# Layer two of a two-layer transformer: sums of key blocks 0 and 1, and of 2 and 3, of the second query half made in pairs

## The chip, the cores and the metric

The kernel runs on one NeuronCore of one Trainium2 chip. The metric is the device time of one execution in microseconds (us), given as the median of several runs. Engines: PE is TensorE (PEld its weight loads), DVE is VectorE, ACT is ScalarE, POOL is GpSimd, SP is SyncE, which here issues DMAs.

## What is computed

Two layers, each an attention and a feed-forward part with a residual sum and a layer normalisation behind each. The change concerns the attention of layer two, which in short is this (two sequences of 1024 tokens, width 512, and per sequence 16 pairs of heads with 16 dimensions):

```python
scores = einsum('bhqd,bhkd->bhqk', q, k) * HD ** -0.5
scores = where(causal, scores, finfo.min)
probs = softmax(scores)
attn_out = einsum('bhqk,bhkd->bhqd', probs, v)
attn = attn_out[:, 0::2] - lambda_full * attn_out[:, 1::2]
```

So each of the 32 heads (16 in each of 2 sequences) has two components, each with scores of its own, that share one v of 32 columns.

## The kernel before

Layer two runs at 1621 to 2209 us of the span. A projection makes q, k and v, then 32 heads follow in `attention_phase` (called with `L1`).

**Work of a head.** The 1024 queries are two halves of 512 (`qc`), the keys eight blocks of 128 (`kt`). Under the causal mask the first half has key blocks 0 to 3 and the second 0 to 7, so there are 12 steps (`L.steps`): 0 to 3 for the first half, 4 to 11 for the second. Step 4 is key block 0 of the second half, steps 5, 6, 7 are blocks 1, 2, 3; steps 4 to 8 have all 512 queries, steps 9 to 11 have 384, 256 and 128. For each step and component:

- `score` (L626): a matmul with 50 rows, scores with keys down and queries across, into one of 3 banks of PSUM (`p_work`), taken in turn;
- `exp` on ACT (L816), into one of 4 probability buffers (`prob`, in `l_w_hi`);
- for the diagonal blocks (steps 0 to 3 and 8 to 11) POOL sets masked places to zero (L572);
- `sum_up` (L646): four products, v and a column of ones for both components, each into 32 columns of the array, added up in PSUM over the steps of a query half. TensorE runs each in two passes, so that a sum is 8 weight loads and 8 matmuls.

ACT copies the sums of a half (L769), TensorE turns them (`turn`, L696), DVE divides and combines.

**Maxima.** Before a head's scores are made, its queries' maxima must be known: `pair` (L604) makes scores with 48 rows the other way round into one of 4 banks (`p_ring`), and DVE reduces them (L883 without a mask; L880 with it, whose result is read out by a short second instruction). A head has 12 units of one 512-key piece or less, for 2 components: 24 matmuls and 24 reductions. TensorE makes them one to two heads ahead. DVE turns their maxima into a shift (L890), TensorE transposes it (`turn_shift`, L612), DVE copies it out (L897, L899). Turned sums and shifts use the banks of `p_ring` too.

Scores and maxima of component 0 use rows 0 to 63 of the array, those of component 1 rows 64 to 127. Below, a *score group* is an unbroken run of scores and maxima, which lies between sums or turns.

**Waits.** Every bank that is used again costs a wait, which stands ahead of the matmul on TensorE's one instruction stream:

```python
L593  pe.wait_ge(freed, L.freed_at[older])         # a maximum: the one 4 banks ago is reduced
L622  pe.wait_ge(exped, at - SCORE_BANKS + 1)      # a score: the one 3 banks ago is through exp
L640  pe.wait_ge(exped, 2 * (step + 1))            # sums of steps 4 to 7
L636  pe.wait_ge(out_copied, QC * n + qc)          # step 4: the first half's sums are copied
```

ACT's exp of step s waits for the sums of step s - 4 of the sequence (its buffer).

**Order.** A string of letters sets TensorE's order for each head (`Layer.heads`): Q and R take the next maxima of component 0 and 1, P both; U, V take the next score (components in turn), S two; W takes the next sum; X is the shift, T a turn. Sums run two steps behind the scores at the start of the string. DVE takes the maxima, shifts and turns in TensorE's order, ACT the exps in the order of the scores.

In the string before, the 5th to the 8th W are steps 4, 5, 6, 7, with a score group ahead of each: `WWW UUQRVQ W RUR W X QRUQUV W RUQUV W` (the first three W are steps 1 to 3, the X is a shift).

Of the kernel before, what the change touches and what calls it, by code (L numbers as in the profile page):

```python
# [31 lines left out]
B, T, D = 2, 1024, 512  # L32
# [50 lines left out]
class Layer:  # L83
# [141 lines left out]
    def k_head(self, n):  # L225
# [3 lines left out]

L0 = Layer("l0", D, D, False, "QRUWUQURUQDRUUUQRWUQUURQDRUUQRUWQUURUQWRUUQDXTWRUUUQRDQUURQUWRUUQURWQUURQUWRUU",  # L230
           24, (6, 12, 26))
L1 = Layer("l1", D // 4, D // 4, True, "PVRWSQVTQRVUVRWWWUUQRVQWRURWXQRUQUVWRUQVWUVURQRQWTQVRVUWWWQUV",
           20, (3, 2))


# [1318 lines left out]
def program(nc, A, out):  # L1554
    dram = lambda n, s, d: nc.dram_tensor(n, s, d, kind="Internal").ap()
    q_parts = [dram(f"q_parts{l}", (B * D // HD, PARTS * HD, T), F32) for l in range(2)]
    k_parts = [dram(f"k_parts{l}", (B * L.k_dims // HD, PARTS * HD, T), F32) for l, L in enumerate((L0, L1))]
    x0 = A["L0_attn_x"].rearrange("b t d -> (b t) d")
    out = out.rearrange("b t d -> (b t) d")
    with ExitStack() as ctx:  # L1560
# [60 lines left out]
        with ExitStack() as layer:  # L1621
            wo1_hi = layer.enter_context(nc.sbuf_tensor("wo1_hi", [P, KD, D], F32R))
            v_sb = layer.enter_context(nc.sbuf_tensor("v_all1", [P, NT * L1.v_dims], F32))
            early = ExitStack()
            early_q = early.enter_context(nc.sbuf_tensor("early_q", [P, 2, T], F32R))
            early_k = early.enter_context(nc.sbuf_tensor("early_k", [P, 1, T], F32R))
            wo = (wo_stage, Split(wo1_hi, wo_area.taken_by("wo_lo1", [P, KD, D], F32R)))
            attention_phase(nc, L1, xT, q_parts[1], k_parts[1], v_sb, attn_area, 2 * H_SIZE, neg_lambda[1][:, 0:1], C,
                            early_q[:, :, :], early_k[:, :, :], mean_sq, wo, norm_w[:, 1:2], [])
# [41 lines left out]
```

## Time and profile before

| | us |
|---|---|
| median of 3 runs | 2338.39 (2336.61 to 2339.71) |
| profiled execution, its own time | 2330.37 |
| its span, first to last instruction | 2328.6 |
| around the span | 1.8 |
| PE busy | 2240.8 (96%) |
| DVE busy | 1589.4 (68%) |
| ACT busy | 1241.2 (53%) |
| sums of layer two (L646), first to last start | 1673.5 to 2207.7 |

Busy time of an engine is the union of its instructions' spans; shares are of the span. The matmuls' spans are pipelined (each lasts on while later ones have started), so a PE at 100% is one without a visible hole. What a matmul or a sum costs is read from one start to the next start.

### The profile page before, as it was taken

The numbers are of one execution on the slowest core, as the hardware profiler recorded it, in microseconds if no ns is written. First come the engines' busy times: TensorE is split into PE (matmuls) and PEld (weight loads), VectorE is DVE, ScalarE is ACT, GpSimd is POOL, SyncE is SP. The second block draws the span as 40 slices with busy tenths as digits, with TensorE's granted clock in tenths as the row PEclk, the third lists the DMA queues.
The fourth block names the chain that finished last, engine by engine and source line by source line (L and its number), as shares of the span: only waits on it lengthen the run. The fifth ranks groups of instructions, "written<-read, shape, count | busy, mean of one in ns | idle before, by whom it ended". The sixth has DMA issues, their size and how long they took to land. (4 is left out here: it accounts for less than half of the span.)

```text
span 2328.6 us, 42022 instructions
## 1 busy us (share of the span) xinstructions
PE 2240.8 (96%) x14576; PEld 1292.5 (56%) x14576; DVE 1589.4 (68%) x3629; ACT 1241.2 (53%) x2486; POOL 930.9 (40%) x767
## 2 busy tenths in 40 slices
PE   8898999999999999799999999978999999999999
PEld 6663333333333333578888888857644444444377
DVE  3247899999999995554444443462589898889567
ACT  3116778787878787341222212251366666666644
POOL 4007888889999999510000000001011212121152
PEclk9999999999999999899999999989999999999989
DMA  6654322242223000220000000004702321220011
GB/s 221 154 131 52 83 29 29 29 55 30 29 29 51 7 2 2 69 73 28 1 27 27 27 27 27 1 1 127 153 14 37 44 43 29 37 44 2 2 46 55
DMA packets 59001, 109.00 MB, mean 47 GB/s; under 512 B 12028, under 2 KB 23292, under 8 KB 58808
## 3 DMA queue, kind: packets, MB, share of 16 engines
q1 hardware_dynamic: 57960, 103.39, 21.4%
q0 software_dynamic: 848, 3.15, 0.4%
q8 instruction: 107, 1.75, 0.3%
q14 instruction: 86, 0.70, 0.1%
HBM read 73.75 MB, written 31.46 MB: 45 GB/s over the span
## 5 line engine op out<-in xcount | busy, mean ns | idle before, releaser
L883 DVE TENSOR_REDUCE l_maxima<-l_p_ring 128x1 f32<-128x512 f32 x1280 | 814.2, 685 | 90.7 <-PE l_p_ring L604 73.3
L816 ACT ACTIVATE l_w_hi_prob<-l_p_work 128x512 f32<-128x512 f32 (+3 forms) x1280 | 600.1, 535 | 217.4 <-PE l_p_work L626 211.8
L604 PE MATMUL l_p_ring<-xT_all 48*128 48x512 f32 (+3 forms) x1680 | 490.8, 419 | 0.0
L626 PE MATMUL l_p_work<-xT_all 50*128 50x512 f32 (+3 forms) x1680 | 471.3, 417 | 0.0
L604 PEld LDWEIGHTS l_p_ring<-xT_all 48*128 48x128 f32 x1680 | 243.7, 186 | 334.2 <-DVE l_maxima L883 204.8
L558 POOL TENSOR_TENSOR l_part<-l_w_hi_prob,l_w_hi_prob 128x1024 f32<-128x1024 f32 x128 | 304.4, 2379 | 186.6 <-ACT l_w_hi_prob L816 147.7
L572 POOL TENSOR_SCALAR_AFFINE_SELECT l_w_hi_prob<-l_w_hi_prob 128x256 f32<-128x256 f32 x256 | 105.7, 419 | 515.8 <-ACT l_w_hi_prob L816 515.8
L558 POOL TENSOR_TENSOR l_part<-x_prob,x_prob 128x1024 f32<-128x1024 f32 x128 | 302.1, 2383 | 20.5 <-ACT x_prob L816 20.0
L626 PEld LDWEIGHTS l_p_work<-xT_all 50*128 50x128 f32 x1680 | 234.9, 185 | 130.0 <-ACT l_w_hi_prob L816 85.4
L816 ACT ACTIVATE x_prob<-l_p_work 128x512 f32<-128x512 f32 x512 | 275.3, 601 | 50.8 <-PE l_p_work L626 50.7
L646 PE MATMUL l_p_work<-l_w_hi_prob,v_all 128*32 128x512 f32 (+3 forms) x1536 | 301.3, 497 | 0.3 <-ACT l_w_hi_sums L769 0.2
L646 PE MATMUL l_p_work<-l_w_hi_prob,l_ones 128*32 128x512 f32 (+3 forms) x1536 | 301.1, 497 | 0.0
L880 DVE CUSTOM_DVE_ANT_0 l_masked_scores<-l_p_ring,l_mask 128x128 bf16<-128x128 f32 (+3 forms) x512 | 235.7, 487 | 49.4 <-PE l_p_ring L604 43.2
L1457 DVE SCALAR_TENSOR_TENSOR ffn_h<-ffn_p_u,ffn_group_scales,ffn_silu 128x512 f32<-128x512 f32 x64 | 48.1, 751 | 204.9 <-PE ffn_p_u L263 193.8
L1255 POOL TENSOR_SCALAR ffn_w<-ffn_w 128x1024 f32<-128x1024 int32 x21 | 24.2, 1174 | 409.0 <-DMA ffn_w<-in_L_ffn_down_w_T 409.0
L682 PE MATMUL l_p_ring<-l_part,l_ones 128*32 128x512 f32 x1024 | 136.9, 607 | 5.8 <-POOL l_part L558 5.8
L662 PE MATMUL l_p_work<-x_prob,v_all 128*32 128x512 f32 x1024 | 137.8, 611 | 0.0
L662 PE MATMUL l_p_work<-l_w_hi_prob,v_all 128*32 128x512 f32 x1024 | 137.4, 608 | 0.1
L1398 ACT ACTIVATE ffn_silu<-ffn_p_g,ffn_group_scales 128x512 f32<-128x512 f32 x64 | 44.0, 687 | 175.2 <-PE ffn_p_g L263 175.2
L1402 ACT ACTIVATE attn_h_hi<-ffn_h 128x512 fp32r<-128x512 f32 x64 | 40.4, 632 | 166.7 <-DVE ffn_h L1457 166.7
L960 DVE TENSOR_TENSOR l_part<-l_p_work,l_part 128x512 fp32r<-128x512 f32 x52 | 35.8, 691 | 135.7 <-ACT l_part L833 135.7
L646 PEld LDWEIGHTS l_p_work<-l_w_hi_prob,v_all 128*32 128x32 f32 x1536 | 70.6, 109 | 103.3 <-issue 57.9
(169 smaller groups left out, 3688.0 us busy)
## 6 DMA issues: line engine op xcount, KB each, us to landing
xT_all<-q_parts SPq DMA_DIRECT2D x180, 128.0 KB
q_parts<-l_part SPq DMA_DIRECT2D x64, 256.0 KB
xT_all<-k_parts SPq DMA_DIRECT2D x90, 128.0 KB
k_parts<-l_part SPq DMA_DIRECT2D x40, 256.0 KB
xT_all<-k_parts SPq DMA_DIRECT2D x90, 64.0 KB
ffn_w<-in_L_ffn_gate_w_T SPq DMA_DIRECT2D x8, 512.0 KB, 3.7
ffn_w<-in_L_ffn_up_w_T SPq DMA_DIRECT2D x8, 512.0 KB, 4.6
ffn_w<-in_L_ffn_down_w_T SPq DMA_DIRECT2D x8, 512.0 KB, 5.5
```

Source lines behind the costliest of these rows:

```text
L558: pool.tensor_tensor(pairs[room], prob[(step - QC) % L.prob_ring][:, :, :], prob[step % L.prob_ring][:, :, :], ALU.add).then_inc(paired, 1)
L572: pool.affine_select(out=part, in_=part, compare_op=ALU.is_ge, fill=0.0, base=0, pattern=[[0, 2], [1, P]], channel_multiplier=-1).then_inc ...
L604: filling = pe.matmul(p_ring[:, L.bank_at["maxima", n, u, sub] % L.ring, 0:keys], q[i][rows, n % 2, qt * P:(qt + 1) * P], k[i][rows, L.k_h ...
L626: pe.matmul(p_score[:, at % SCORE_BANKS, off:CH], k[i][rows, L.k_head(n), kt * P:(kt + 1) * P], q[i][rows, n % 2, qc * CH + off:(qc + 1) * ...
L646: summing = pe.matmul(p_out[r0:r0 + VD, off:CH], lhs, prob[step % L.prob_ring][:, sub, off:CH], start=first, stop=final)
L662: summing = pe.matmul(p_out[r0:r0 + VD, :], v, prob[(n * S + QC * kt + qc) % L.prob_ring][:, sub, :], start=kt == 0, stop=kt == KT - 1)
L682: summing = pe.matmul(p_ones[r0:r0 + VD, :], ones[:, :], added[:, sub, :], start=p == 0, stop=p == ONES_ROUNDS - 1)
L816: act.activation(prob[step % L.prob_ring][:, sub, off:CH], p_score[:, at % SCORE_BANKS, off:CH], ACT.Exp, scale=HD ** -0.5).then_inc(exped, 1)
L880: dve.tensor_tensor_reduce(masked_scores[sub][:, 0:keys], scores, mask[:, CH - keys:CH], 1.0, MASKED, ALU.add, ALU.max, to).then_inc(freed, 1)
L883: dve.tensor_reduce(to, scores, AX.X, ALU.max).then_inc(freed, 1)
L1398: act.activation(silu[i % 2][:, :], p_g[:, i % 2, :], ACT.Silu, scale=group_scales[par][:, 0, i:i + 1]).then_inc(silu_done, 1)
L1457: dve.scalar_tensor_tensor(out=h_full[i % 2][:, :], in0=p_u[:, i % 2, :], scalar=group_scales[par][:, 1, i:i + 1], in1=silu[i % 2][:, :], ...
```

## The change

One string is different: in each head, the sum of step 4 moves behind the following score group, to step 5, and that of step 6 moves behind the following group, to step 7.

```diff
-L1 = Layer("l1", D // 4, D // 4, True, "PVRWSQVTQRVUVRWWWUUQRVQWRURWXQRUQUVWRUQVWUVURQRQWTQVRVUWWWQUV",
+L1 = Layer("l1", D // 4, D // 4, True, "PVRWSQVTQRVUVRWWWUUQRVQRURWWXQRUQUVRUQVWWUVURQRQWTQVRVUWWWQUV",
            20, (3, 2))
```

No instruction is added or dropped: the rows of DVE, ACT, POOL and SP stay as they were, and on PE 2 of 12 sums a head move (16 of its weight loads, 16 of its matmuls).

TensorE around step 4 in a head of layer two (`l1_p_ring` are the maxima's banks, `l1_p_work` those of scores and sums, `l1_w_hi_prob0` and `prob1` the probabilities of steps 4 and 5; four rows of L646 are one sum):

```order
 L604 MATMUL l1_p_ring<-xT1_all_50,xT0_all_49 128x128
-L646 MATMUL l1_p_work<-l1_w_hi_prob0_20010,v_all1 32x512
-L646 MATMUL l1_p_work<-l1_w_hi_prob0_20010,l1_ones 32x512
-L646 MATMUL l1_p_work<-l1_w_hi_prob0_20010,v_all1 32x512
-L646 MATMUL l1_p_work<-l1_w_hi_prob0_20010,l1_ones 32x512
 L604 MATMUL l1_p_ring<-xT1_all_50,xT0_all_49 128x256
 L626 MATMUL l1_p_work<-early_q,early_k 128x512
 L604 MATMUL l1_p_ring<-xT1_all_50,xT0_all_49 128x384
+L646 MATMUL l1_p_work<-l1_w_hi_prob0_20010,v_all1 32x512
+L646 MATMUL l1_p_work<-l1_w_hi_prob0_20010,l1_ones 32x512
+L646 MATMUL l1_p_work<-l1_w_hi_prob0_20010,v_all1 32x512
+L646 MATMUL l1_p_work<-l1_w_hi_prob0_20010,l1_ones 32x512
```

The sum of step 4 now stands behind two maxima (256 and 384 keys) and the score of step 7, component 0; the sum of step 5 follows it at once.

TensorE around steps 6 and 7 of the same head (`prob2` holds the probabilities of step 6):

```order
+L604 MATMUL l1_p_ring<-xT1_all_50,xT0_all_49 128x512
+L626 MATMUL l1_p_work<-early_q,early_k 128x384
+L604 MATMUL l1_p_ring<-xT1_all_50,xT0_all_49 128x512
+L626 MATMUL l1_p_work<-early_q,early_k 128x384
 L646 MATMUL l1_p_work<-l1_w_hi_prob2_20012,v_all1 32x512
 L646 MATMUL l1_p_work<-l1_w_hi_prob2_20012,l1_ones 32x512
 L646 MATMUL l1_p_work<-l1_w_hi_prob2_20012,v_all1 32x512
 L646 MATMUL l1_p_work<-l1_w_hi_prob2_20012,l1_ones 32x512
-L604 MATMUL l1_p_ring<-xT1_all_50,xT0_all_49 128x512
-L626 MATMUL l1_p_work<-early_q,early_k 128x384
-L604 MATMUL l1_p_ring<-xT1_all_50,xT0_all_49 128x512
-L626 MATMUL l1_p_work<-early_q,early_k 128x384
```

Two maxima of 512 keys and both scores of step 9 (384 queries) now come ahead of the sum of step 6 and join the group before it; the sum of step 7 follows that of step 6.

## Rows read from the trace of the kernel before

**Rows 1.** Busy time by stage: us, busy (x count) of each engine, granted clock, DMA.
```profile
1650.00:1700.00 50.00, 45.08 (x298) 25.83 (x300) 29.86 (x97) 19.92 (x45) 4.90 (x12) 0.90 0.60 110
1900.00:2000.00 100.00, 100.00 (x936) 44.49 (x928) 89.53 (x302) 68.91 (x163) 19.85 (x48) 1.00 0.25 38
```

**Rows 2.** Timeline of PE, one head, steps 4 and 5: start, us, line, operation.
```profile
1900.26 0.50 PE L626 MATMUL l_p_work<-xT_all 50*128 50x512 f32 x2
...
1900.66 0.44 PE L626 MATMUL l_p_work<-xT_all 50*128 50x512 f32 x1
1900.84 0.22 PE L604 MATMUL l_p_ring<-xT_all 48*128 48x128 f32 x1
1901.05 0.62 PE L646 MATMUL l_p_work<-l_w_hi_prob,v_all 128*32 128x512 f32 x1
...
1902.04 0.38 PE L604 MATMUL l_p_ring<-xT_all 48*128 48x256 f32 x1
1902.05 0.49 PE L626 MATMUL l_p_work<-xT_all 50*128 50x512 f32 x1
1902.27 0.33 PE L604 MATMUL l_p_ring<-xT_all 48*128 48x384 f32 x1
1902.53 0.62 PE L646 MATMUL l_p_work<-l_w_hi_prob,v_all 128*32 128x512 f32 x1
...
1903.41 0.38 PE L612 MATMUL l_p_ring<-ident,l_shift 128*16 128x128 f32 x2
```

**Rows 3.** Timeline of PE, the same head, steps 6 and 7.
```profile
1903.72 0.56 PE L604 MATMUL l_p_ring<-xT_all 48*128 48x256 f32 x3
1904.07 0.63 PE L626 MATMUL l_p_work<-xT_all 50*128 50x512 f32 x3
1904.62 0.62 PE L646 MATMUL l_p_work<-l_w_hi_prob,v_all 128*32 128x512 f32 x1
...
1905.62 0.49 PE L604 MATMUL l_p_ring<-xT_all 48*128 48x512 f32 x1
...
1905.95 0.34 PE L626 MATMUL l_p_work<-xT_all 50*128 50x384 f32 x1
1906.23 0.62 PE L646 MATMUL l_p_work<-l_w_hi_prob,v_all 128*32 128x512 f32 x1
...
1907.22 0.39 PE L626 MATMUL l_p_work<-xT_all 50*128 50x256 f32 x2
```

**Rows 4.** Timeline of PE, the next head, up to its step 4.
```profile
1914.53 0.50 PE L604 MATMUL l_p_ring<-xT_all 48*128 48x512 f32 x2
1914.87 0.63 PE L626 MATMUL l_p_work<-xT_all 50*128 50x512 f32 x3
1915.11 0.40 PE L604 MATMUL l_p_ring<-xT_all 48*128 48x512 f32 x1
1915.44 0.51 PE L646 MATMUL l_p_work<-l_w_hi_prob,v_all 128*32 128x384 f32 x1
...
1917.65 0.62 PE L646 MATMUL l_p_work<-l_w_hi_prob,v_all 128*32 128x512 f32 x1
```

**Rows 5.** Timeline of ACT, the head of rows 2: copy of sums, then exps.
```profile
1900.39 0.60 ACT L769 ACTIVATE l_w_hi_sums<-l_p_work 128x512 f32<-128x512 f32 x1
1900.89 0.59 ACT L816 ACTIVATE l_w_hi_prob<-l_p_work 128x512 f32<-128x512 f32 x1
...
1904.50 0.60 ACT L816 ACTIVATE l_w_hi_prob<-l_p_work 128x512 f32<-128x512 f32 x1 [1.25 <-PE l_p_work L626]
1904.99 0.59 ACT L816 ACTIVATE l_w_hi_prob<-l_p_work 128x512 f32<-128x512 f32 x1
```

**Rows 6.** Timeline of DVE, the same head: where reductions with a mask are read out.
```profile
1901.74 0.08 DVE L880 DVE_READ_ACCUMULATOR2_ANT l_maxima<- 128x1 f32 x1
...
1905.04 0.08 DVE L880 DVE_READ_ACCUMULATOR2_ANT l_maxima<- 128x1 f32 x1
```

**Rows 7.** Timeline of PE's weight loads, the third score of rows 2.
```profile
1900.60 0.19 PEld L626 LDWEIGHTS l_p_work<-xT_all 50*128 50x128 f32 x1
```

## The prediction

> **What bounds the kernel now.** I read the busy time by stage first, to see which engine sets the pace of layer two's heads. In 100 us of it PE is busy for 100.00, DVE for 89.53 and ACT for 68.91, at a granted clock of 1.00 (2.4 GHz) [rows 1]. Then the timeline of PE: the sum of step 4 starts at 1901.05 and again at 1917.65, so a head takes 16.60 us [rows 2, 4], and 32 of them some 531 us. PE has no hole that shows, so a head's time is the sum of what PE's instructions cost from start to start, and only what shortens PE's stream or puts a wait into it counts. The timelines of ACT and DVE, read last, say when a bank comes free; the reader is to hold those times against the starts on PE.
>
> **What is saved: two changes of work a head.** A sum that a score group follows takes 0.99 us (1901.05 to 1902.04; 1906.23 to 1907.22), one that the shift follows, which is of the same kind (narrow columns), 0.88 (1902.53 to 1903.41) [rows 2, 3]. So a sum that another sum follows is worth 0.88, 0.11 less. A group pays at both its ends: a 512-wide matmul costs 0.34 as the first of its half of the array (1914.53 to 1914.87), 0.24 in the middle (to 1915.11) and 0.33 as the last (to 1915.44) [rows 4], which is 0.10 and 0.09 for the ends. A pair of sums in place of two single ones thus saves 0.11 + 0.10 + 0.09 = 0.30 us. Two pairs in each of 32 heads: 19 us, if nothing waits. The Trainium skill has the reason for these ends, in TensorEngine Tiling (Array Packing), Key Properties: a change of tiling mode drains TensorE. The rows agree with it, and by that rule alone the time would fall by the 19 us; that is the first rival.
>
> **What is added: the sums were the cover of waits.** Today a single sum stands between two score groups and lasts about 1 us, in which DVE reduces maxima and ACT takes exps out of the banks that the next group wants. The change takes that 1 us away ahead of both groups; what waits stands ahead of everything else on PE's one stream, both sums included. I work out each place by its last wait. Prices: from the end of the work that frees something to PE's start 0.06, as the sum of step 4 shows, which waits for the copy that ends at 1900.39 + 0.60 = 1900.99 and starts at 1901.05 [rows 2, 5]; from a weight load within a group to its matmul 0.06 (1900.60 to 1900.66) [rows 7, 2].
>
> *Step 4.* Its group now runs on: 256-key maximum, score of step 7 (component 0), 384-key maximum. If nothing waited, they would follow the 128-wide maximum of 1900.84 within some 0.2 us. But:
> - the score of step 7 uses the bank of the score of step 5, component 1, whose exp ends at 1900.89 + 0.59 = 1901.48 [rows 5];
> - the 384-key maximum uses the bank of the last 512-key maximum made before the 128-wide ones, which DVE has read out at 1901.74 + 0.08 = 1901.82 [rows 6]. This wait ends last.
>
> Both are set by earlier PE work that stays where it is, and DVE works without a hole there, so the change does not hasten them. The matmul starts at 1901.82 + 0.06 + 0.06 = 1901.94. From it to the sum behind it today's 0.26 (1902.27 to 1902.53) [rows 2] holds: sum of step 4 at 1902.20, step 5 at 1903.08, the shift at 1903.96, where it is 1903.41 now. **0.55 us later.**
>
> *Step 6.* I count from the start of the shift, S, as the reductions and exps there follow from work behind S. The group today starts at S + 0.31 (1903.72) with three maxima and three scores [rows 3]; the two maxima and two scores of the next one now join it. The last two must wait:
> - the second 512-key maximum for the bank of the 256-key one behind the shift, read out at 1905.04 + 0.08 = 1905.12, S + 1.71 [rows 6];
> - the first score of step 9 for the exp of step 7, component 1, which ends at 1904.50 + 0.60 = 1905.10, S + 1.69; the second for that of step 8, component 0, which ends at 1904.99 + 0.59 = 1905.58, S + 2.17 [rows 5]. This ends last.
>
> The second score starts at S + 2.17 + 0.06 + 0.06 = S + 2.29; with today's 0.28 from it to the sum (1905.95 to 1906.23) [rows 3] the sum of step 6 starts at S + 2.57, step 7 at + 3.45, and with 0.99 the next group at S + 4.44. Today that is 1907.22 - 1903.41 = S + 3.81. **0.63 us later.**
>
> So a head is 0.55 + 0.63 = 1.18 us longer, the saving included. Once PE is later, the waits in the rest of the head become shorter, and none is on its path today; nothing gives the loss back, and PE's steps behind keep their lengths. Of 32 heads I count 31, since in the last one no maxima are left to be made and the first of the two waits is a lighter one: 31 x 1.18 = 36.6, taken as **+36 us**.
>
> What costs nothing: the instructions are the same ones. The exps of steps 8 and 10 wait for the sums of steps 4 and 6, which now end later; but the first exp of step 8 would start at about S + 1.58 (1904.99 - 1903.41), long behind the sum of step 4, and scores of step 10 come only behind step 7's sum. The copy of the first half's sums is no longer waited for (a few hundredths, inside the working). DVE and POOL wait for nothing that moved later than their own banks, and SP's queue has nothing moved past it.
>
> **Bounds.** Below: with neither the 0.06 of the wake-up nor that of the load the places give 0.43 and 0.51, 29 us. Above: if a load behind a wait costs as much as one at a group's start, 0.10 (above), and one more wake-up falls in each place, it is 0.10 more in each, 1.38 a head, 43 us. I take the middle, since its prices are those of a wait and a load in this very place.
>
> Against its own time the profiled execution would go from 2330.4 to 2366; the median of the runs shown lies 8.0 above it, which gives 2374.
>
> **Rivals.**
> 1. *It gets faster.* The saving stands and the banks come free in time: 2338.4 - 19 = 2319. That needs PE to pass a waiting score and run the sums, or DVE and ACT to be ahead. For it: halves of the array do pass one another (three maxima start from 1903.72, the third of which is behind a score in the program, and the scores only from 1904.07) [rows 3]. Against it: that is passing what waits for its half, not for a semaphore, and the last reads of both places lie some 0.8 us and more behind the time at which the group wants the bank; DVE at 90% has no such lead [rows 1]. It decides at 0.55 and 0.63 us: if the frees came earlier by more than these, the kernel would be faster. Chance 0.06. On the other side the Trainium skill says in TensorEngine Tiling (Array Packing), PSUM Bottleneck, that tiling hastens TensorE and not the emptying of PSUM, which may then be the bound. By it the change has nothing to gain in either place; the rows of DVE and ACT above agree.
> 2. *One place only.* One of the two waits is covered, for instance because PE's delay in one place gives DVE and ACT a lead in the other. The covered place then saves its 0.30, or comes out even where half a wait is left: a head is longer by 0.25 to 0.33, or by 0.55 to 0.63, 31 of them by 8 to 20 us: 2346 to 2358. For it: DVE is idle a little ahead of the shift's copies. Against it: the last wait of the second place is ACT's, counted from the shift itself. Chance 0.08.
> 3. *The two cancel.* Waits of 0.30 where I work out 0.85 to 0.93: no change, 2338. No row gives such a value. Chance 0.03.
> 4. *The clock falls too.* PE now stands still for up to half a microsecond four times a head. In the stage ahead of the heads, where PE is busy for 45.08 of 50 us, the granted clock is 0.90, a mixture of both levels (1.2 and 2.4 GHz) [rows 1]. A clock of 0.97 would add 3% of 531 us, 16 us: 2390. Against it: the holes are short beside those of that stage. Chance 0.04.
>
> **How the numbers follow.** The forecast has 0.79; its own range is 2367 to 2381. Rival 2 at its upper end and half of what lies between are taken in below, a little of rival 4 above: 2355 to 2384 leaves out rival 1, rival 3, the lower part of rival 2 and rival 4, together near 0.2. A measurement of this kernel can tell some 0.2%, 5 us, from no change. Faster by more: 0.07. Within: 0.03. Slower: 0.90.
>
> **What would show it.** In the profile after: a head takes 17.7 to 17.8 us instead of 16.60; the sums of steps 4 and 5 start 0.88 apart, those of 6 and 7 too; ahead of the sum of step 4 the last 384-key maximum starts 0.1 us behind a read-out on DVE, and ahead of step 6 the last score the same behind the exp of step 8; DVE's and ACT's shares of the heads fall to about 84% and 64%; the clock stays at 1.00. I am wrong if the head takes under 16.6, if those two matmuls start long behind what frees their banks, or if DVE's reductions ahead of step 4 start earlier against the turn than now.

## The result and the profile after

The changed kernel takes 2372.12 us (median of 6 runs, 2366.56 to 2377.3), against 2337.4 (2332.98 to 2339.71, 6 runs) for the kernel before in the same comparison: a ratio of 1.0146, 95% interval [1.0128, 1.0165]. It is slower by 34.7 us; 2374 was forecast, with a range of 2355 to 2384.

The profiled execution after took 2374.88 us, with a span of 2373.1; its busy time by engine, from the page of the profile:

```profile
PE 2277.5 (96%) x14576; PEld 1321.9 (56%) x14576; DVE 1589.6 (67%) x3629; ACT 1237.9 (52%) x2486; POOL 931.4 (39%) x767
```

Busy time by stage, 100 us of the heads, to hold against [rows 1]:

```profile
1900.00:2000.00 100.00, 98.27 (x858) 46.07 (x854) 83.80 (x284) 64.58 (x154) 17.72 (x43) 1.00 0.24 36
```

DVE has as much work in all as before (1589.6 us against 1589.4), but in 100 us of the heads it does 83.80 where it did 89.53, and ACT 64.58 where it did 68.91: fewer heads fit into the stretch. PE's 100.00 has become 98.27; the waits only just show as holes, since matmuls' spans overlap. The clock is 1.00 as before.

PE's timeline around steps 4 and 5 of one head after, to hold against [rows 2] (start, duration, line, operation):

```profile
1905.27 0.22 PE L604 MATMUL l_p_ring<-xT_all 48*128 48x128 f32 x1
1905.70 0.38 PE L604 MATMUL l_p_ring<-xT_all 48*128 48x256 f32 x1 [0.17 <-DVE l_maxima L880]
1905.97 0.50 PE L626 MATMUL l_p_work<-xT_all 50*128 50x512 f32 x1
1906.31 0.44 PE L604 MATMUL l_p_ring<-xT_all 48*128 48x384 f32 x1
1906.68 0.62 PE L646 MATMUL l_p_work<-l_w_hi_prob,v_all 128*32 128x512 f32 x1
...
1907.56 0.59 PE L646 MATMUL l_p_work<-l_w_hi_prob,v_all 128*32 128x512 f32 x1
...
1908.42 0.38 PE L612 MATMUL l_p_ring<-ident,l_shift 128*16 128x128 f32 x2
```

Before, the 128-wide maximum was followed by the sum of step 4 after 0.21 us [rows 2]. Now three matmuls stand in that place, each on its own (x1) and each late: from 1905.27 to the sum at 1906.68 it takes 1.41 us.

Steps 6 and 7 of the same head behind the shift of 1908.42, to hold against [rows 3], and the next head's step 4, to hold against [rows 4]:

```profile
1910.16 0.44 PE L626 MATMUL l_p_work<-xT_all 50*128 50x384 f32 x1
...
1910.65 0.44 PE L626 MATMUL l_p_work<-xT_all 50*128 50x384 f32 x1
1911.02 0.62 PE L646 MATMUL l_p_work<-l_w_hi_prob,v_all 128*32 128x512 f32 x1
...
1911.90 0.59 PE L646 MATMUL l_p_work<-l_w_hi_prob,v_all 128*32 128x512 f32 x1
...
1912.87 0.39 PE L626 MATMUL l_p_work<-xT_all 50*128 50x256 f32 x2
...
1924.51 0.62 PE L646 MATMUL l_p_work<-l_w_hi_prob,v_all 128*32 128x512 f32 x1
```

The head takes 1924.51 - 1906.68 = 17.83 us. What frees the banks, from DVE's timeline, the two read-outs ahead of step 4, to hold against [rows 6]:

```profile
1905.57 0.08 DVE L880 DVE_READ_ACCUMULATOR2_ANT l_maxima<- 128x1 f32 x1
...
1906.18 0.08 DVE L880 DVE_READ_ACCUMULATOR2_ANT l_maxima<- 128x1 f32 x1
```

and from ACT's timeline, the exp that frees the bank of step 7's score, and those of steps 7 and 8, to hold against [rows 5]:

```profile
1905.33 0.59 ACT L816 ACTIVATE l_w_hi_prob<-l_p_work 128x512 f32<-128x512 f32 x1
...
1909.51 0.60 ACT L816 ACTIVATE l_w_hi_prob<-l_p_work 128x512 f32<-128x512 f32 x1 [1.83 <-PE l_p_work L626]
1910.00 0.59 ACT L816 ACTIVATE l_w_hi_prob<-l_p_work 128x512 f32<-128x512 f32 x1
```

Put ends beside starts: the read-outs end at 1905.65 and 1906.26, and the 256-key and 384-key maxima start at 1905.70 and 1906.31. The exp of step 5 ends at 1905.92, and the score of step 7 starts at 1905.97. The exps of steps 7 and 8 end at 1910.11 and 1910.59, and the two scores of step 9 start at 1910.16 and 1910.65. Five matmuls, each 0.05 to 0.06 us behind what frees its bank. Over the heads the median from the end of the freeing work to the start is 0.055, 0.053, 0.055, 0.053 and 0.053 us for the five; before it was 0.83, 0.57, 0.44, 0.52 and 0.37. Each bank used to be free long ahead of its use. (A sixth, the first of the 512-key maxima that joined the second group, starts 0.11 behind the copies of the shift; a later wait covers it.)

The change seen over the heads, as medians of the time from a head's first sum (step 0) to the start of a later one, worked out from the starts of L646 and L612 in PE's timeline:

| us from the sum of step 0 to | before | after | later by |
|---|---|---|---|
| sum of step 4 | 5.19 | 6.39 | 1.20 |
| sum of step 5 | 6.68 | 7.28 | 0.60 |
| shift | 7.56 | 8.13 | 0.57 |
| sum of step 6 | 8.77 | 10.72 | 1.95 |
| sum of step 7 | 10.37 | 11.61 | 1.24 |
| the group behind step 7 | 11.37 | 12.58 | 1.21 |
| the next head | 16.61 | 17.83 | 1.22 |

Up to step 3 and behind step 7 nothing moves. The first place costs 0.57 us, the second 0.64, and no more falls elsewhere.

### The profile page after: what moved, and what is told of

It reads as the page before. It is cut to its first block and busy times, and to the rows that moved or that the text cites. A ratio compares the mean times of both kernels' runs of the same rounds, so it can differ in the third digit from the quotient of the medians.

```text
span 2373.1 us, 42022 instructions
## 1 busy us (share of the span) xinstructions
PE 2277.5 (96%) x14576; PEld 1321.9 (56%) x14576; DVE 1589.6 (67%) x3629; ACT 1237.9 (52%) x2486; POOL 931.4 (39%) x767
## 3 DMA queue, kind: packets, MB, share of 16 engines
q8 instruction: 107, 1.75, 0.3%
## 5 line engine op out<-in xcount | busy, mean ns | idle before, releaser
L604 PE MATMUL l_p_ring<-xT_all 48*128 48x512 f32 (+3 forms) x1680 | 503.6, 421 | 4.9 <-DVE l_maxima L880 4.9
L626 PE MATMUL l_p_work<-xT_all 50*128 50x512 f32 (+3 forms) x1680 | 477.7, 418 | 5.3 <-ACT l_w_hi_prob L816 2.0
L646 PE MATMUL l_p_work<-l_w_hi_prob,v_all 128*32 128x512 f32 (+3 forms) x1536 | 289.3, 496 | 0.2 <-ACT l_w_hi_sums L769 0.2
L646 PE MATMUL l_p_work<-l_w_hi_prob,l_ones 128*32 128x512 f32 (+3 forms) x1536 | 289.3, 496 | 0.0
L646 PEld LDWEIGHTS l_p_work<-l_w_hi_prob,v_all 128*32 128x32 f32 x1536 | 76.8, 110 | 121.6 <-issue 81.2
```

The source lines that it names most:

```text
L604: filling = pe.matmul(p_ring[:, L.bank_at["maxima", n, u, sub] % L.ring, 0:keys], q[i][rows, n % 2, qt * P:(qt + 1) * P], k[i][rows, L.k_h ...
L626: pe.matmul(p_score[:, at % SCORE_BANKS, off:CH], k[i][rows, L.k_head(n), kt * P:(kt + 1) * P], q[i][rows, n % 2, qc * CH + off:(qc + 1) * ...
L646: summing = pe.matmul(p_out[r0:r0 + VD, off:CH], lhs, prob[step % L.prob_ring][:, sub, off:CH], start=first, stop=final)
```

## The experiments

**One place at a time.** The first kernel moves only the sum of step 4, the second only that of step 6. Against the changed kernel each puts one W back:

```diff
-"PVRWSQVTQRVUVRWWWUUQRVQRURWWXQRUQUVRUQVWWUVURQRQWTQVRVUWWWQUV"
+"PVRWSQVTQRVUVRWWWUUQRVQRURWWXQRUQUVWRUQVWUVURQRQWTQVRVUWWWQUV"
```

> Only the sum of step 4 moves. Theory (each pair pays for its own wait, DVE's read-out ahead of step 4): the shift 0.57 us later than before against the head's first sum, as in the changed kernel (8.13 less 7.56), nothing else moves; a head 17.2 us, 31 x 0.57 = 18 us more, about 2355. Rival (the loss is one thing, for instance the lower cover shared by both places, or the clock): then step 4 alone gives either nearly all of the 35 us or nearly none of it.

```diff
-"PVRWSQVTQRVUVRWWWUUQRVQRURWWXQRUQUVRUQVWWUVURQRQWTQVRVUWWWQUV"
+"PVRWSQVTQRVUVRWWWUUQRVQWRURWXQRUQUVRUQVWWUVURQRQWTQVRVUWWWQUV"
```

> Only the sum of step 6 moves. Theory (the exp of step 8 holds the last score of step 9): from the shift to the group behind step 7 4.45 us instead of 3.81, a head 17.25 us, 31 x 0.64 = 20 us more, about 2357. With the first run the two parts should add up to the whole, 18 + 20 against the 38 us of the profile. Rival (lead of DVE and ACT passes from one place to the other): the parts add up to clearly more than the whole, or one of them is near 0.

Measured: 2353.56 us, ratio 1.0079 [1.0058, 1.0101], a head of 17.19 us for step 4 alone; 2353.78 us, 1.0089 [1.0068, 1.0111], a head of 17.25 for step 6 alone. That is 0.58 and 0.64 more than before, together 1.22, as much as both at once. The places don't help one another: the delay of the first gives DVE and ACT no lead in the second. PE's timeline of the first kernel at its one changed place:

```profile
1898.10 0.44 PE L604 MATMUL l_p_ring<-xT_all 48*128 48x384 f32 x1
1898.47 0.62 PE L646 MATMUL l_p_work<-l_w_hi_prob,v_all 128*32 128x512 f32 x1
...
1899.36 0.59 PE L646 MATMUL l_p_work<-l_w_hi_prob,v_all 128*32 128x512 f32 x1
...
1900.21 0.38 PE L612 MATMUL l_p_ring<-ident,l_shift 128*16 128x128 f32 x2
```

The same distances as with both: 0.37 from the last maximum to the pair, 0.89 and 0.85 for its two sums.

**Which engine is waited for.** In the next two kernels the order is the changed one, and one engine has less work in layer two. First DVE reduces only a quarter of each maximum's keys, so these maxima are those of too few keys, and the mask is read from its start, where it masks nothing of the diagonal:

```diff
+                    if L.causal:
+                        keys = keys // 4
...
-                        dve.tensor_tensor_reduce(masked_scores[sub][:, 0:keys], scores, mask[:, CH - keys:CH], 1.0, MASKED,
+                        dve.tensor_tensor_reduce(masked_scores[sub][:, 0:keys], scores, mask[:, 0:keys], 1.0, MASKED,
```

> The changed kernel, with each reduction of DVE in layer two over the first quarter of its columns alone, and its mask left out (maxima of part of the scores). Theory: the 384-key maximum ahead of step 4 waits for DVE no longer; next in line is the score of step 7 with its wait for an exp, which starts 0.34 us earlier than that maximum does now; so the sum of step 4 starts 0.35 to 0.4 us earlier, step 6 stays as late against the shift as it is (its last wait is ACT's), a head 17.4 to 17.5 us, 11 to 12 us less than the changed kernel. Rival (DVE has no part in it): 17.8 us, no change.

Then ACT makes only a quarter of each exp (the `step` in this edit counts through the whole layer, so all exps are shortened but those of its first 8 steps; the rest of each probability buffer keeps old values):

```diff
-                act.activation(prob[step % L.prob_ring][:, sub, off:CH], p_score[:, at % SCORE_BANKS, off:CH], ACT.Exp,
+                done = off + (CH - off) // 4 if L.causal and step >= 8 else CH
+                act.activation(prob[step % L.prob_ring][:, sub, off:done], p_score[:, at % SCORE_BANKS, off:done], ACT.Exp,
```

> The changed kernel, with each exp of layer two from step 8 of the first head on over the first quarter of its columns alone (the rest of the probabilities are left as they were). Theory: step 4 stays as late as it is, since DVE's read-out is the last wait there; ahead of step 6 the exps are no longer waited for, and the second 512-key maximum with its read-out at 1.71 us behind the shift comes last: the sum of step 6 starts at about 2.15 to 2.2 us behind the shift instead of 2.59, a head 17.4 us, 12 to 13 us less than the changed kernel. Rival (ACT has no part in it): 17.8 us, no change.

With short maxima: 2359.55 us, 1.0119 [1.0098, 1.0140], a head of 17.52. The sum of step 4 stands at 6.10 instead of 6.39, and from the shift to the sum of step 6 nothing changes (2.58 us against 2.59). PE's timeline ahead of step 4, and the row of ACT that frees the score's bank:

```profile
1894.76 0.49 PE L626 MATMUL l_p_work<-xT_all 50*128 50x512 f32 x1 [0.32 <-ACT l_w_hi_prob L816]
1894.76 0.44 PE L604 MATMUL l_p_ring<-xT_all 48*128 48x384 f32 x1
1895.18 0.62 PE L646 MATMUL l_p_work<-l_w_hi_prob,v_all 128*32 128x512 f32 x1
```

```profile
1894.11 0.59 ACT L816 ACTIVATE l_w_hi_prob<-l_p_work 128x512 f32<-128x512 f32 x1
```

The 384-key maximum no longer waits for DVE; it stands behind the score of step 7, and that now is the last wait, 0.06 us behind an exp that ends at 1894.70. Without DVE's wait the first place is thus 0.29 us better off, and what comes last there then is ACT's; the second place does not change.

With short exps: 2361.27 us, 1.0108 [1.0087, 1.0129], a head of 17.42. The other way round: the sum of step 4 stays at 6.39, and from the shift to the sum of step 6 it takes 2.20 us instead of 2.59. PE's timeline ahead of step 6:

```profile
1904.16 0.38 PE L612 MATMUL l_p_ring<-ident,l_shift 128*16 128x128 f32 x2
...
1905.93 0.50 PE L604 MATMUL l_p_ring<-xT_all 48*128 48x512 f32 x1
1905.93 0.44 PE L626 MATMUL l_p_work<-xT_all 50*128 50x384 f32 x1
1906.36 0.62 PE L646 MATMUL l_p_work<-l_w_hi_prob,v_all 128*32 128x512 f32 x1
```

and the row of DVE that frees the maximum's bank:

```profile
1905.79 0.08 DVE L881 DVE_READ_ACCUMULATOR2_ANT l_maxima<- 128x1 f32 x1
```

The score no longer waits for its own bank; it goes together with the second 512-key maximum, 1.77 us behind the shift, which waits for the read-out that ends at 1905.87. So the last wait of each place is the one that the prediction named, and the next one is the other engine's that it listed: an exp of ACT ahead of step 4, a read-out of DVE ahead of step 6.

**Both engines short,** in the changed order and, for comparison, in the order before (the same two edits in either):

> The changed kernel with both: reductions over the first quarter of their columns without a mask, and exps over the first quarter of theirs. Theory: with both consumers short, the two losses go almost wholly (what is left is the way from a score through its exp to the bank's next user, whatever the exp's length); a head 16.6 to 16.9 us against 17.83, about that of the kernel before, and the pairs' own saving begins to show. If each wait stood alone, 0.3 from the short reductions and 0.4 from the short exps, a head would be 17.1; more than that comes off if one wait was hidden behind the other. Rival (the sums in pairs cost time themselves, or the clock does): a head stays over 17.4.

> The kernel before with the same two cuts (reductions and exps over a quarter of their columns). Theory: its sums cover the waits, so PE's stream alone sets the time, and the head stays at 16.6 us; only the last heads' tail may shorten by a few us. Rival (DVE or ACT are a bound of the kernel before as well): a head shorter by more than 0.3 us.

The changed order then takes 2339.07 us, 1.0012 [1.0001, 1.0024] against the whole kernel before, with a head of 16.76; the order before takes 2329.69, 0.9973 [0.9961, 0.9986], with a head of 16.61. Busy time of 100 us of heads, the changed order first:

```profile
1900.00:2000.00 100.00, 99.92 (x918) 46.86 (x912) 49.86 (x297) 35.62 (x161) 18.42 (x47) 1.00 0.27 38
```

```profile
1900.00:2000.00 100.00, 100.00 (x932) 43.62 (x929) 51.30 (x303) 36.09 (x164) 19.47 (x49) 1.00 0.28 38
```

Two things follow. In the order before, DVE at 51.30 instead of 89.53 and ACT at 36.09 instead of 68.91 don't shorten a head by a hundredth (16.607 us against 16.615): neither the reductions nor the exps hold PE up there, which the prediction took from the rows and could not show. (The 0.3% by which this kernel is faster does not show in the heads of its profile; where it comes from is open.) One wait for ACT is in every head of that order all the same: the sum of step 4 starts 0.052 to 0.055 us behind the end of ACT's copy of the first half's sums, in the kernel before ([rows 2, 5], 1900.99 and 1901.05) as in this one, which leaves the copy as long as it was. From the last 128-key maximum to that sum it is 0.21 us, from one to the sum of step 8, which waits for nothing there, 0.15, so this wait costs about 0.06 us a head, an estimate from these two distances.

And in the changed order 1.07 of the 1.22 us go, which were thus waits for DVE and ACT. But the pairs still gain nothing: a head is 0.15 longer than in the order before, 0.08 of it up to the shift and 0.07 from there to the group behind step 7. Waits are left in both places. ACT's timeline ahead of step 4, DVE's, then PE's:

```profile
1889.00 0.60 ACT L769 ACTIVATE l_w_hi_sums<-l_p_work 128x512 f32<-128x512 f32 x1 [0.31 <-PE l_p_work L646]
1889.50 0.44 ACT L817 ACTIVATE l_w_hi_prob<-l_p_work 128x128 f32<-128x128 f32 x2
```

```profile
1889.86 0.08 DVE L883 DVE_READ_ACCUMULATOR2_ANT l_maxima<- 128x1 f32 x1
```

```profile
1889.82 0.49 PE L626 MATMUL l_p_work<-xT_all 50*128 50x512 f32 x1
1890.00 0.43 PE L604 MATMUL l_p_ring<-xT_all 48*128 48x384 f32 x1
1890.36 0.62 PE L646 MATMUL l_p_work<-l_w_hi_prob,v_all 128*32 128x512 f32 x1
```

The exp that frees step 7's bank stands behind ACT's copy of the first half's sums, which itself waits for those sums; the first of the two short exps is 0.27 us long and ends at 1889.77, and the score starts 0.05 behind it. The last wait is DVE's here too: the read-out ends at 1889.94, and the 384-key maximum starts at 1890.00. The sum of step 4 is at 5.90, still 0.71 later than before. In the second place both scores of step 9 start 0.053 to 0.054 us behind their short exps. So the run with both engines short is not one of pairs without waits.

**Can an order with pairs win?** Four orders were written anew from the prices that the runs above had given, one of them a second time with one letter moved; the diffs show each string against that of the kernel before, the moved letter against the string it was moved in. The first two:

```diff
-"PVRWSQVTQRVUVRWWWUUQRVQWRURWXQRUQUVWRUQVWUVURQRQWTQVRVUWWWQUV"
+"TRVSWWVVRQRQUUWWPUUVQWWRRQVUVRXWQVQVVRQWUVRRUQWRUVUQQWWWQRUUT"
```

> The kernel before with another string, in which sums stand in pairs (steps 0 and 1, 2 and 3, 4 and 5) and the scores and maxima between are laid out anew so that few of them come within 1 us of what frees their bank: TRVSWWVVRQRQUUWWPUUVQWWRRQVUVRXWQVQVVRQWUVRRUQWRUVUQQWWWQRUUT. Theory (a pair saves about 0.3 us where no wait takes its place): a head 16.1 to 16.4 us, 7 to 15 us less than before in all. Rival (a pair loses its cover wherever it stands): a head over 16.7, slower than before.

```diff
-"PVRWSQVTQRVUVRWWWUUQRVQWRURWXQRUQUVWRUQVWUVURQRQWTQVRVUWWWQUV"
+"VRQWRQUSTPVVURWWWUQUUQXWWUURRRUQWVVQUQRQWWQVVVRRTVQVUQRWWWVRU"
```

> The kernel before with a third string: the shift moved ahead of step 4, steps 4 and 5 in a pair behind a group without the next head's maxima of 256 and 384 keys, and steps 7 and 8 in a pair: VRQWRQUSTPVVURWWWUQUUQXWWUURRRUQWVVQUQRQWWQVVVRRTVQVUQRWWWVRU. Theory: a head 16.1 to 16.4 us, 7 to 15 us less than before in all. Rival (a pair loses its cover wherever it stands): a head over 16.7, slower than before.

Both missed: 2360.82 us, 1.0103 [1.0083, 1.0124], a head of 17.20; and 2372.68 us, 1.0161 [1.0142, 1.0180], a head of 17.80. In the first, maxima again start 0.055 us behind DVE's read-outs. DVE's row, then PE's ahead of the sum of step 8:

```profile
1903.60 0.08 DVE L880 DVE_READ_ACCUMULATOR2_ANT l_maxima<- 128x1 f32 x1
```

```profile
1903.74 0.50 PE L604 MATMUL l_p_ring<-xT_all 48*128 48x512 f32 x1
1904.16 0.62 PE L646 MATMUL l_p_work<-l_w_hi_prob,v_all 128*32 128x512 f32 x1
```

In the second the shift stands ahead of the pair of steps 4 and 5, and PE stands still for it. The last maximum before it, and the shift; then the row of DVE that it waits for:

```profile
1897.82 0.22 PE L604 MATMUL l_p_ring<-xT_all 48*128 48x128 f32 x1
1899.27 0.28 PE L612 MATMUL l_p_ring<-ident,l_shift 128*16 128x128 f32 x1 [1.23 <-DVE l_shift L890]
```

```profile
1899.03 0.19 DVE L890 TENSOR_REDUCE l_shift<-l_maxima 128x16 f32<-128x32 f32 x1
```

The shift wants the reduction of L890, which stands on DVE behind the last maxima of the head to come. The next kernel moves that one letter behind the pair; two more orders with other places follow.

```diff
-"VRQWRQUSTPVVURWWWUQUUQXWWUURRRUQWVVQUQRQWWQVVVRRTVQVUQRWWWVRU"
+"VRQWRQUSTPVVURWWWUQUUQWWXUURRRUQWVVQUQRQWWQVVVRRTVQVUQRWWWVRU"
```

> The order of the run before with one letter moved: the shift stands behind the sums of steps 4 and 5 instead of ahead of them. If the 1.23 us in which TensorE stood ahead of the shift were what made that order slow, they vanish: a head takes 17.80 - 1.23 = 16.6 us or a little less, the kernel is within 0.5% of the kernel before, and no place ahead of the shift's transposes shows a hole. If other waits were hidden behind that hole, they come to light at the next place that wants a bank, and a head stays over 17.2 us (over 1% slower).

```diff
-"PVRWSQVTQRVUVRWWWUUQRVQWRURWXQRUQUVWRUQVWUVURQRQWTQVRVUWWWQUV"
+"QRVWUVURQTRSUWWWVQUPVQWWRUQVRRVXWVQVQRUWQRURUVWWUQRQUVTWWVQUR"
```

> An order written out anew, in which sums stand in runs of three or two but maxima are spread so that each bank's last reduction lies about two sums back. By the prices of the runs so far (matmul 0.05 us behind what frees its bank, 0.37 us from a lone last matmul to the sum, 0.30 us saved by each pair) a head would take 16.1 to 16.4 us and the kernel 2322 to 2332, faster by 0.3 to 0.6%. If every order that pairs the sums ends on a wait for DVE, a head takes 17.0 us or more and the kernel is slower by 0.6% or more.

```diff
-"PVRWSQVTQRVUVRWWWUUQRVQWRURWXQRUQUVWRUQVWUVURQRQWTQVRVUWWWQUV"
+"RPUWUVQRUTURSWWWRRQUVVQWWQRUVQVRXWURQVVQWVVQVRRWTUQVURQWWWQUU"
```

> A second order of that kind, with other places for the pairs. Same expectation by the prices: a head of 16.2 to 16.5 us, the kernel 2325 to 2335, faster by 0.1 to 0.5%. By the other theory (pairs always end on a wait for DVE): a head of 17.0 us or more, slower by 0.6% or more.

The moved shift gives 2346.23 us, 1.0044 [1.0028, 1.0061], and a head of 16.86: within the 0.5% that was expected, though not at 16.6. 0.94 of the 1.23 us come back, and the shift follows its pair without a hole (0.86 us behind the pair's second sum). The hole was the largest part; what stays above 16.6 stands with other waits, three of them for DVE, which bind in every head (two maxima ahead of step 7 at 0.055 us behind a read-out, one ahead of step 1 at 0.095), and two for ACT's copies (the sums of steps 0 and 4 at 0.053).

The last two orders come out even: 2337.16 us, 1.0003 [0.9989, 1.0017], a head of 16.55, and 2339.71 us, 1.0012 [1.0000, 1.0025], a head of 16.58. Neither expectation holds. The pair of steps 4 and 5 waits for no bank in either (each bank ahead of it is free 0.21 us or more before its use), so "pairs always wait for DVE" is refuted; but both have 7 runs of sums a head where the kernel before has 8, which at 0.30 us should have given 16.31. They gain 0.06 and 0.03. In the first order the missing 0.24 us is about what one wait behind step 7 costs, DVE's row and then PE's:

```profile
1909.61 0.08 DVE L880 DVE_READ_ACCUMULATOR2_ANT l_maxima<- 128x1 f32 x1
```

```profile
1909.25 0.50 PE L604 MATMUL l_p_ring<-xT_all 48*128 48x512 f32 x2
1909.59 0.28 PE L626 MATMUL l_p_work<-xT_all 50*128 50x256 f32 x1
1909.74 0.32 PE L604 MATMUL l_p_ring<-xT_all 48*128 48x128 f32 x1
1909.75 0.49 PE L626 MATMUL l_p_work<-xT_all 50*128 50x128 f32 x2
1910.17 0.62 PE L646 MATMUL l_p_work<-l_w_hi_prob,v_all 128*32 128x512 f32 x1
```

The read-out ends at 1909.69 and the maximum of 128 keys starts 0.05 later. The group takes 0.92 us; the second order has one of the same six widths ahead of step 8, without a wait, and there it takes 0.66, 0.26 less.

In the second order no score or maximum starts less than 0.18 us behind the freeing of its bank. What binds there is a wait that the list ahead of the prediction leaves out: the first score of a head (L624) waits until the shift has come through DMA. From the trace's waits (us in total where a hole shows, times, longest), then SP's timeline, then PE's around that score:

```profile
PE l_p_work L626 <- DMA xT_all<-l_shift_rows: 5.4, 12, 1.1
```

```profile
1908.40 2.63 SPq L415 DMA_DIRECT2D xT_all<-l_shift_rows  x4
```

```profile
1911.83 0.32 PE L626 MATMUL l_p_work<-xT_all 50*128 50x128 f32 x1
...
1912.29 0.50 PE L626 MATMUL l_p_work<-xT_all 50*128 50x512 f32 x2
...
1912.91 0.51 PE L646 MATMUL l_p_work<-l_w_hi_prob,v_all 128*32 128x384 f32 x1
```

The last of the four transfers lands at 1912.15, and the score starts 0.135 us behind it, in every steady head alike (in the kernel before it is 1.63 in the median). This group takes 1.08 us, where one with as much work in the fuller half of the array took 0.78 without a wait (the first order, ahead of its turn): 0.30 more. Without these two waits the heads would be about 16.29 and 16.28, close to the 16.31; this is an estimate from the groups named, and no run shows it. (The first score waits for the DMA in the same way in the first of the four orders, that of 17.20 us.) No order that was tried beats the kernel before by more than the measurement can tell.

## Why the prediction was right

**The bound.** Neither DVE's reductions nor ACT's exps hold PE up in the heads before: shown by the kernel of the order before with short maxima and exps, whose head is as long. That no wait at all is on PE's path, as the prediction has it, is not quite so: the sum of step 4 waits for ACT's copy in every head, for about 0.06 us. In the changed order this sum comes 1.25 us behind the copy.

**The saving.** A sum followed by a sum was to cost 0.88; it does at its first place in each pair (1906.68 to 1907.56, 1911.02 to 1911.90). The 0.19 for a group's two ends also shows in groups of the kernel before that wait for nothing: those ahead of steps 5, 7, 0 and 1 last 0.49, 0.61, 0.85 and 0.91 us, with 1.25, 1.75, 2.75 and 3.00 times 512 columns in the fuller half of the array, which is 0.19 us and 0.24 for each 512. That the saving exists beneath the waits was not seen alone: each of the orders with pairs has a wait that binds somewhere in the head. With both engines short 1.07 of 1.22 us go, and in the last two orders the pair's 0.30 is missing by about what one wait costs.

**Step 4.** Forecast 0.55 us, measured 0.57 with both and 0.58 alone. The last wait is the one named, DVE's read-out. It ends at 5.97 us from the head's first sum (1906.26 against a sum of step 4 at 6.39 and 1906.68), and in [rows 6] at 5.96 (1901.82 against 5.19 and 1901.05): the change did not hasten DVE, as assumed.

**Step 6.** Forecast 0.63, measured 0.64. The exp of step 8 was to end at S + 2.17, counted from the shift, and does (1910.59 - 1908.42). The sum of step 6 was to start at S + 2.57 and starts at S + 2.60.

**Two prices inside were off, in opposite directions.** I took 0.12 from the freeing to the matmul's start (0.06 for the wait, 0.06 for the load) and 0.26 or 0.28 from there to the sum. Measured are 0.05 and 0.37. PE's weight load of the waiting maximum, after:

```profile
1906.31 0.18 PEld L604 LDWEIGHTS l_p_ring<-xT_all 48*128 48x128 f32 x1 [0.16 <-DVE l_maxima L880]
```

Load and matmul have the same start in the trace, 1906.31; the load is inside the matmul, which lasts 0.44 where it lasted 0.33 with its weights loaded ahead [rows 2]. The load so costs 0.11 rather than 0.06, but later than I put it. The two errors leave 0.04 in the first place and 0.02 in the second; the second sum of a pair is 0.02 shorter than forecast (0.86 instead of 0.88 ahead of the shift, 0.97 instead of 0.99 ahead of a group) and takes that back in part.

**The sum.** 31 times 1.18 was 36.6. From the first step-0 sum to the last step-11 sum it is 572.6 us against 534.0, 38.6 more, nearly 32 times 1.22: the last head pays as much as the others (14.82 us from its first sum to its last against 13.59), where I had left it out as the lighter one. It has no maxima, but the score of step 7 waits there for ACT's exp (0.053 us behind it). The profiled execution is 44.5 us longer than the one before, and the 6 us beyond the heads lie ahead of them: the first sum of layer two starts at 1680.1 instead of 1673.5, where no instruction of the change stands. The medians, 34.7 us apart, don't show them, so I don't count them to the change. They are also 3.9 us less apart than the heads of the two profiles, which is no more than executions of one kernel differ by (2332.98 to 2339.71 before): that the forecast 2374 meets the median to 2 us, while the heads were forecast 2 us too short, is in part luck.

**The rivals.** Faster: out, since all five matmuls wait and the sums behind them wait along. The Trainium skill, TensorEngine Tiling (Array Packing), PSUM Bottleneck, has the emptying of PSUM as what may become the bottleneck once tiling has hastened TensorE. The trace agrees in both places (0.05 us behind the reductions and exps). One place only: out, since both pay in full and their costs add up. The two cancel: out, a head is 1.22 us longer. The clock: 1.00 in the heads in spite of PE's waits. The shares forecast, 84% for DVE and 64% for ACT, are 83.80 and 64.58.

## What to carry to other kernels

Work on the bounding engine that looks like an interruption may be the cover of another engine's latency: before two pieces of it are joined, look up for each instruction that then comes earlier when the bank that it wants comes free, and hold that against its new start. A saving per change of work is only had if no such wait is later than the new start, and the last wait is what counts, the second to last standing close behind it. Here an engine at 90% and one at 69%, whose reductions and exps never held up the third, each cost it half a microsecond a head once the third asked 1 us earlier. And a list of waits has to be whole: in one order it was a wait for a DMA, on no list, that took a pair's saving.

## What the runs showed of the hardware that was not expected

- A matmul that waits for a semaphore starts 0.053 to 0.055 us after the work that frees it ends, its weight load starting along with it; the load shows in the matmul's own length (0.44 against 0.33 us for 384 columns).
- The distance from a lone last matmul of a group to the sum behind it is 0.37 us, against 0.26 for one whose weights were loaded ahead.
- A matmul may start before an earlier one that uses other rows of the array ([rows 3] show three maxima ahead of a score), but none was seen to pass one that waits for a semaphore. In the kernel with short maxima the 384-key maximum of component 1 starts at 1894.76 together with the waiting score of component 0, though DVE's last read-out before that ends at 1894.55; in the kernel with short exps the score of component 1 starts at 1905.93 together with the waiting maximum of component 0, though its own bank was free 0.24 us before. So the other half of the array is no way around a wait, which is what the first rival would have needed.
- The shift's way through DMA takes long beside a head: SP issues its four transfers one behind the other (2.63 us), and in the last order the score that wants them starts 5.73 us behind the shift's matmul, 0.135 us behind the last landing.
